# Decoder kernel, expert phase: a deeper row ring, one VectorE job behind each tile, and a scatter split around GpSimd's inverses

## The reference

```python
scores = feats @ centroids.T                       # 8192 rows, 8 experts
expert = jnp.argmax(scores, axis=1)
alpha = sigmoid(sum(feats * centroids[expert]))
h = (xs - mu) * rsqrt(var + 1e-5) * g + b          # per expert, xs = feats
y = xs + relu(h @ W1e.T + b1e) @ W2e.T + b2e       # hidden width 512
out = alpha * y[expert] + (1.0 - alpha) * feats
x = _layernorm(x + out)                            # the kernel's result
```

## Time and profile before

| what | value |
|---|---|
| median of three runs | 3524.48 us |
| the profiled execution | 3520.38 us |
| its span in the profile | 3518.5 us |
| granted TensorE clock over the span | 0.959 |
| start of the expert phase in the span | about 3302 us |

### The profile page before, as it was taken

How to read it: one execution, slowest core, us unless ns; L and a number is a source line. 1 busy time by engine, 2 the same in 40 slices (tenths; PEclk the granted TensorE clock), 3 DMA queues, 4 the chain that set the end, 5 groups by cost and what they waited for, 6 DMA issues and landing times. The chain is left out here.

```text
span 3518.5 us, 101747 instructions
## 1 busy us (share of the span) xinstructions
PE 3132.9 (89%) x40973; PEld 1931.2 (55%) x40973; DVE 2410.5 (69%) x5699; ACT 1967.9 (56%) x3510; POOL 2064.2 (59%) x1842
## 2 busy tenths in 40 slices
PE   6888888877999999898999999999999989999676
PEld 2433444433555556665666666665555545666575
DVE  5999999994555555585665556677888855666465
ACT  5666666652566666432666654335555536666354
POOL 5888888884787877663111114556777742343365
PEclk8999999998999999998999998999999989999798
DMA  4222222225600000000000000000000000000364
GB/s 143 103 90 91 96 100 92 89 88 195 217 2 2 2 2 2 16 1 13 4 5 5 5 3 6 8 8 2 2 2 2 2 17 24 21 17 14 98 175 116
DMA packets 50327, 165.42 MB, mean 47 GB/s; under 512 B 11822, under 2 KB 23217, under 8 KB 40784
## 3 DMA queue, kind: packets, MB, share of 16 engines
q1 hardware_dynamic: 45520, 150.43, 13.1%
q0 software_dynamic: 4352, 8.47, 0.7%
HBM read 149.89 MB, written 43.65 MB: 55 GB/s over the span
## 5 line engine op out<-in xcount | busy, mean ns | idle before, releaser
L530 DVE TENSOR_TENSOR_SCAN XC<-ssm_dA,ssm_db 128x2048 f32<-128x2048 f32 x128 | 565.2, 4416 | 55.6 <-PE ssm_db L374 55.6
L479 ACT ACTIVATE ssm_dA<-ssm_delta,ssm_nega 128x508 f32<-128x508 f32 x512 | 326.0, 707 | 165.9 <-DVE XC L530 162.6
L1229 POOL TENSOR_TENSOR self_pm<-self_pT,weights 128x512 f32<-128x512 f32 x256 | 322.6, 1294 | 54.4 <-ACT self_pT L953 53.0
L594 POOL TENSOR_TENSOR XC<-XC,XB 128x1536 f32<-128x1536 f32 x64 | 253.3, 3958 | 87.9 <-DVE XC L530 87.9
L1235 POOL TENSOR_TENSOR XC<-XC,XB 128x128 f32<-128x128 f32 x128 | 58.5, 458 | 391.6 <-DVE XB L1111 391.6
L594 POOL TENSOR_TENSOR ssm_hC<-XC,XB 128x1536 f32<-128x1536 f32 x64 | 251.8, 3934 | 36.6 <-DVE XC L530 36.6
L374 PE MATMUL ssm_db<-XB,ssm_dxT 32*128 32x128 f32 x4096 | 157.0, 292 | 103.3 <-DVE XC L530 88.9
L374 PEld LDWEIGHTS ssm_db<-XB,ssm_dxT 32*128 32x128 f32 x4096 | 131.7, 193 | 203.8 <-DVE XC L530 183.9
L1097 DVE TENSOR_REDUCE self_nmax<-self_scores 128x4 f32<-128x512 f32 x256 | 158.0, 679 | 82.0 <-PE self_scores L830 81.8
L2663 POOL TENSOR_TENSOR XC<-XC,weights 128x512 f32<-128x512 f32 x128 | 161.8, 1285 | 73.1 <-ACT XC L2497 73.1
L2671 POOL TENSOR_TENSOR XC<-XC,weights 128x512 f32<-128x512 f32 x128 | 161.4, 1283 | 49.7 <-ACT XC L2506 49.5
(11 more groups left out here) (454 smaller groups left out, 8354.3 us busy)
## 6 DMA issues: line engine op xcount, KB each, us to landing
XB<-c_rows SPq DMA_DIRECT2D x64, 1024.0 KB
sorted<-in_padding SPq DMA_DIRECT2D x1, 33280.0 KB, 109.2
experts_we<-in_w_experts SPq DMA_DIRECT2D x72, 323.0 KB, 3.1
experts_rt<-sorted SPq DMA_DIRECT2D x72, 65.0 KB
ssm_xT<-in_xT SPq DMA_DIRECT2D x16, 256.0 KB
XC<-in_w_experts SPq DMA_DIRECT2D x9, 256.0 KB
weights<-in_w_self SPq DMA_DIRECT2D x1, 1412.0 KB, 7.3
cross_ctx_t<-in_ctx SPq DMA_DIRECT2D x16, 77.0 KB
```

The costliest lines, as they stand in the source:

```text
L479: o = act.activation(dA[:, p % 2, :].rearrange("p (b k t) -> p b k t", b=GROUP, k=4)[:, :, k, 1:T], by_batch(delta[:, slot, half, :])[:, : ...
L530: dve.tensor_tensor_scan(states(p).rearrange("p m t -> p (m t)"), dA[:, p % 2, :], db[:, :], 0.0, ALU.mult, ALU.add).then_inc(h_ready, 1)
L594: pool.tensor_tensor(weighted(p).rearrange("p (b k) t -> p b k t", k=4)[:, :, 0:3, :], states(p).rearrange("p (b k) t -> p b k t", k=4)[:, ...
L1229: pool.tensor_tensor(pm[:, n % 2, r, :].rearrange("p (h t) -> p h t", h=4), pT[:, n % 2, r, :].rearrange("p (h t) -> p h t", h=4), bcast(V ...
```

## The change

The ring of fetched rows holds six quads in place of four, and rows are fetched four quads ahead in place of three. The index tile `idx` gets a ring of its own, of eight quads. VectorE's four jobs are spread over the quad: `head_a(q + 2)` behind tile 0, `finish_b(q - 1)` behind tile 1, `head_b(q + 2)` behind tile 2, `finish_a(q)` behind tile 3. On GpSimd the fourth transfer of a quad leaves the burst: it is issued one iteration later, between inverse r and inverse z, and the three others stay behind inverse z.

```diff
--- before.py
+++ after.py
@@ -2693,7 +2693,8 @@
     line = table.rearrange("r w -> (r w)")
     HALVINGS = NB.bit_length() - 1
     assert NB == 1 << HALVINGS
-    RT = 4
+    RT = 6
+    IR = 8
     WS = 8
     HS = 3
     small = w.at["w2"][0]
@@ -2709,7 +2710,7 @@
         tile_at = env["tile_at"]
         alpha = ph.sb("alpha", [P, RT, GROUP])
         rt = ph.sb("rt", [P, RT, GROUP, W])
-        idx = ph.sb("idx", [P, RT, GROUP], U32)
+        idx = ph.sb("idx", [P, IR, GROUP], U32)
         statz = ph.sb("statz", [P, 2, GROUP, 6])
         statr = ph.sb("statr", [P, 2, GROUP, 6])
         mvz = ph.sb("mvz", [P, 2, GROUP, 2])
@@ -2753,7 +2754,7 @@
                 sp.dma_start(rt[:, q % RT, b, :], line[bass.ds(place[j] * (P * W), P * W)].rearrange("(p w) -> p w", w=W)).then_inc(rt_in[q % RT], 16)
 
             place = {}
-            for q in range(3):
+            for q in range(4):
                 for j in range(q * GROUP, (q + 1) * GROUP):
                     locate(j)
                     fetch(j)
@@ -2763,9 +2764,9 @@
             for j in range(TILES):
                 if j + WS < TILES:
                     weights(j + WS)
-                if j + 3 * GROUP < TILES:
-                    locate(j + 3 * GROUP)
-                    fetch(j + 3 * GROUP)
+                if j + 4 * GROUP < TILES:
+                    locate(j + 4 * GROUP)
+                    fetch(j + 4 * GROUP)
             for s in range(2):
                 sp.wait_ge(stored[s], 16 * GROUP * (QUADS // 2))
 
@@ -2857,9 +2858,9 @@
             def head_a(q):
                 dve.wait_ge(rt_in[q % RT], 16 * GROUP * (q // RT + 1))
                 row_stats(dve, lambda b: rt[:, q % RT, b, 0:C], statz[:, q % 2], mvz[:, q % 2], vec_z, q * 2 * GROUP, mark)
-                if q >= RT:
-                    dve.wait_ge(stored[q % 2], 16 * GROUP * ((q - RT) // 2 + 1))
-                dve.tensor_copy(idx[:, q % RT, :], rt[:, q % RT, :, C + 1]).then_inc(idx_ready, 1)
+                if q >= IR:
+                    dve.wait_ge(stored[q % 2], 16 * GROUP * ((q - IR) // 2 + 1))
+                dve.tensor_copy(idx[:, q % IR, :], rt[:, q % RT, :, C + 1]).then_inc(idx_ready, 1)
 
             def head_b(q):
                 dve.wait_ge(pool_z, 2 * q + 2)
@@ -2896,13 +2897,13 @@
                 dve.wait_ge(y_mm, j + 1)
                 dve.scalar_tensor_tensor(r(q % 2)[:, b, :], yp[j % 2][:, 0:C], gate_, here_, ALU.mult, ALU.add)\
                     .then_inc(r_ready, 1)
+                if b == 0 and q + 2 < QUADS:
+                    head_a(q + 2)
                 if b == 1 and q:
                     finish_b(q - 1)
-                if b == 1 and q + 2 < QUADS:
-                    head_a(q + 2)
+                if b == 2 and q + 2 < QUADS:
+                    head_b(q + 2)
                 if b == 3:
-                    if q + 2 < QUADS:
-                        head_b(q + 2)
                     finish_a(q)
             finish_b(QUADS - 1)
 
@@ -2927,11 +2928,11 @@
                     pool.wait_ge(res_ready, q - 1)
                 inv(mvr[:, q % 2], rstdr[:, q % 2], pool_r, q, EPS / 4)
 
-            def scatter(q):
+            def scatter(q, tiles):
                 pool.wait_ge(res_ready, q + 1)
                 pool.wait_ge(idx_ready, q + 1)
-                for b in range(GROUP):
-                    pool.indirect_dma_start(out, bass.IndirectOffsetOnAxis(ap=idx[:, q % RT, b:b + 1], axis=0),
+                for b in tiles:
+                    pool.indirect_dma_start(out, bass.IndirectOffsetOnAxis(ap=idx[:, q % IR, b:b + 1], axis=0),
                                             res(q % 2)[:, b, :], None, bounds_check=NB * P - 1, oob_is_err=False)\
                         .then_inc(stored[q % 2], 16)
 
@@ -2940,12 +2941,15 @@
             for q in range(QUADS):
                 if q:
                     finish(q - 1)
+                if q >= 2:
+                    scatter(q - 2, (3,))
                 if q + 2 < QUADS:
                     head(q + 2)
                 if q:
-                    scatter(q - 1)
+                    scatter(q - 1, (0, 1, 2))
             finish(QUADS - 1)
-            scatter(QUADS - 1)
+            scatter(QUADS - 2, (3,))
+            scatter(QUADS - 1, range(GROUP))
```

## The result

The changed kernel takes **3493.47 us** (median of 4 runs, 3488.87 to 3495.0), beside 3522.41 us for the kernel before (4 runs): a ratio of 0.9919, 95% interval [0.9904, 0.9934]. The forecast was 3488 us. The span of the profiled execution is 3490.8 us.

The account below looks back on a forecast made before the run. Two waits, VectorE's for TensorE and GpSimd's for VectorE, filled 10.52 us iterations; 8.2 (SyncE) over 15 gave -34.8, the last two -2: -37 from 3520.4 made 3483.5, plus 4.1 for the median, 3488 us; range 3479 to 3509.

Parts of the forecast that it names:

- likeliest case: Expert phase: an iteration of 7.97 to 8.6 us, saving 40 to 31 us, so 3484 to 3494 us; chance 65%.
- first rival: Bursts of three still delay TensorE's signals and VectorE waits: 8.8 to 9.96 us an iteration, 3499 to 3516 us; chance 17%.
- Shortening one alone would win little: VectorE's r wait for TensorE (2.65 us) and GpSimd's inverse z wait for VectorE (2.54 to 2.8) close at the same moment.
- instead of 8.2: Iteration of the expert phase: from 10.52 us to SyncE's occupied time, 8.2, over 15 iterations: -34.8 us.
- hidden but for a few tenths: VectorE's r: TensorE's signal, up to 2.3 us late, is mostly covered by VectorE's jobs, now one behind each tile.
- 3.1 us of cover: From r of tile j - 2 VectorE asks for TensorE's result two jobs and one tile later; worst case wants 3.4.
- The three transfers need `finish_b`: GpSimd's burst: its normalisation is made while inverse z is computed, so GpSimd can run without idle time, 7.97 us.
- its stretches double: Rival: each of two bursts an iteration stretches SyncE's instructions as one did, 9.8 us an iteration, 3514 us; chance 5%.
- the single transfer brings late signals of its own: Rival, slower: VectorE is held twice an iteration, 12.3 us, +26 us or 3551 us; chance 6%.
- GpSimd's floor: GpSimd's iteration without idle time: 1.57 + 1.12 + 1.61 + 3.67 = 7.97 us for inverses and transfers.
- third rival: VectorE's normalisations hold GpSimd for their whole length through the shared port: 9.1 us an iteration, 3503 us; chance 3%.
- the forecast's 2: Last two iterations: the single transfer fills 1.12 us of GpSimd's wait for VectorE, once each: -2 us.

Follow-up runs that it names:

- e_three_banks: The changed kernel with three PSUM output banks instead of two, so TensorE may run one tile further ahead: ratio 0.9876 to before, 8.12 us an iteration.
- a_split_only: The changed kernel (deeper rings and fetch, split burst) with VectorE's jobs in their old order: ratio 0.9924 to before, 9.40 us an iteration.
- b_jobs_only: The changed kernel (deeper rings and fetch, new VectorE order) with GpSimd's burst of four back: ratio 0.9975 to before, 10.02 us an iteration.
- g_in_order: The changed kernel with GpSimd's indirect transfers replaced by plain ones in tile order, writing rows to wrong places: one run, 3469.06 us, 7.61 us an iteration.
- m_in_order_again: The changed kernel with plain transfers in tile order, repeated on a fourth chip: one run, 3478.01 us, 7.65 us an iteration.

## Why the prediction was right, and where its terms were off

**Right in sign and in both savings, wrong about what is left.** The forecast was 37 us less and 29 came, which lies just inside its likeliest case (3484 to 3494). Both halves of it took their part: inverse z no longer waits for VectorE, and half of what VectorE waited for TensorE lies behind its jobs. But neither SyncE nor GpSimd bounds the iteration, as it had it; the ring through the late signal does, which is its first rival. Two of its own signs of being wrong stand in the trace, r still waiting over 1 us for TensorE in every iteration and GpSimd idle before its three transfers, and 8.64 us lies just outside its 7.97 to 8.6. The total is right partly by luck: 3493.5 us is as near to the 3499 of the first rival as to its own 3488.

The sentence "Shortening one alone would win little" was wrong: the split alone gave 19.8 us, the order alone 5.9. The burst is a term of the one ring that holds both waits, and the split shortens it.

**The iteration: 8.64 us instead of 8.2.** This term is off by 0.44 x 15 = 6.6 us, of the 8 us missing. Two steps of it were too small.
- *"I take it that the lateness is hidden but for a few tenths."* 1.25 us stay, nearly one half of 2.65. The forecast counted 3.1 us of cover from the moment the bank is free (r of tile j - 2), as if TensorE began the group at once. By the rows of one iteration VectorE asked even later, at 3389.71, 3.7 us behind that r (3386.02), but TensorE began only at 3388.07, 2.05 us behind it, since its groups stand in a queue. The cover that counts is from the group's end, 3389.13, to VectorE's asking, 0.58 us; the lateness was 1.9. So the first rival, half of the lateness exposed (8.8 us), was nearer to what happened inside the iteration than the forecast's own step. Its 8.8 is 0.16 too much since VectorE's work and gaps are 8.64 - 1.25 = 7.4 us and not 7.66.
- *"The three transfers need `finish_b`, which comes one tile later, while inverse z is computed."* It ends while inverse z does (3394.40 and 3394.44), but a transfer starts 0.80 us behind the normalisation that it waited for, 0.20 behind GpSimd's own instruction. 0.57 us an iteration, which no term held. It is no second loss: both stand in one ring, in which the late r pushes the normalisation.

**SyncE: right in size, wrong as the bound.** It waits 0.6 of 8.64 us, so it is occupied for about 8.0, forecast 8.2; with 8.12 an iteration in e_three_banks it still waited. It never decided. The rival that its stretches double fell with that, and so did the one that the single transfer brings late signals of its own: r waits for TensorE once an iteration, as before.

**GpSimd's floor** of 7.97 us was 0.13 too low. The power of z, which now stands beside a normalisation, took 1.14 us on average over 14, that of r 1.04:

```profile
L2917 POOL TENSOR_TENSOR experts_rstdz<-experts_rstdz,experts_power 128x4 f32<-128x4 f32 x14 | 16.0, 1143 | 1.2
L2917 POOL TENSOR_TENSOR experts_rstdr<-experts_rstdr,experts_power 128x4 f32<-128x4 f32 x14 | 14.6, 1043 | 1.2
```

That is the third rival's price: 0.1 us, not 1.1. The power of z (3393.27 to 3394.44) and a whole normalisation of 1.11 us (3393.29 to 3394.40) ran side by side. The Trainium skill ("SBUF — State Buffer", SBUF: two separate sides) says that VectorE in a two-port mode and GpSimd lock one port pair for a whole instruction and that the other fully blocks. No run here shows such a block, though no row tells whether the normalisation ran in that mode.

**The last two iterations** gave 0.7 us instead of 2: 9.03 + 6.87 = 15.9 after 16.57. The split alone took them to 13.74 (a_split_only), the new order alone to 18.27 (b_jobs_only), both on a chip with late signals; where none was late they took 13.87 (e_three_banks) and 13.75 (g_in_order). So the forecast's 2 were in the split, and VectorE's new order, which the forecast gave no term here, took most of them back; why it does so only where signals are late is not shown.

**The start and the clock.** The later weights cost nothing in total, as forecast (25.5 us to the first inverse r), though ScalarE did wait for them once, 2.10 us at 3329.71. The stretches at 1.2 GHz that the forecast allowed for did not come: the granted clock is 1.00 from 3320 to 3460.

**The larger rings** cost nothing, but they are not the free extra that the forecast made of them: in d_three_ahead, with the quads of rows back at four and the fetch at three ahead, the phase is 0.9 us longer than before the change. The forecast asked when the statistics would be wanted, and not whether their rows would be there.

**What is open.** Why the second chip held no signals; whether it is the chip or the loading of the program (on no chip did both kinds show among the kernels with indirect transfers, which speaks for the chip); and what the kernel before and the changed kernel take there, since neither was profiled on it (of before its median there is 3517.91 us, elsewhere 3520.11 to 3526.57). So the share of the third bank in e_three_banks' 8.12 us is not known either: where signals are held it is zero.

## What to carry to other kernels

Count the cover of a late signal from the end of the work that it reports to the moment when the waiting engine would ask, and not from when a buffer comes free. An order that moves a consumer earlier needs its inputs fetched earlier by as much; try the order without the deeper fetch before calling the fetch free. And repeat the winner beside its rival on the same chip: a kernel that by its ratio to before was 0.4% ahead on one chip was level on the next, and only the pair told that.

## What the runs showed of the hardware

- TensorE's signals are held while GpSimd issues a burst of indirect transfers, mostly by 2.3 us before and 1.9 us after the change (2.3 at most) and by some 3.3 us in b_jobs_only, and the r that waits starts mostly 0.8 to 1.0 us behind the burst's end (1.3 at most). This was so in nine profiles on at least three chips, and in neither of the two profiles with such bursts on one other chip. SyncE's instructions stretch with it. The plainest sign is the MOVE ahead of a fetch, 0.03 us at the median: it reaches 0.71 us in the changed kernel and 0.04 in e_three_banks (below, source line L2754 from 3335 to 3435: least, median and most in ns), and in all nine profiles some register instruction of SyncE took 0.70 us or more, in the other five none over 0.16. A long DMA instruction is no such sign: e_three_banks has one of 1.69 us.

```profile
L2754 SPq MOVE experts_rt<-sorted x47: 6/29/711, 3336.3 to 3434.4; - x47
```

```profile
L2754 SPq MOVE experts_rt<-sorted x49: 29/29/37, 3336.3 to 3429.6; - x49
```

- GpSimd's plain transfers of the same tiles take 0.62 us, and three in a row 1.70, where indirect ones took 1.10 and 3.66; no signal was held beside them in g_in_order, whose lines these are, nor in m_in_order_again:

```profile
3384.41 1.70 POOL L2936 DMA_DIRECT2D out<-XB  x3 [0.50 <-DVE XB L141]
...
3389.47 0.62 POOL L2936 DMA_DIRECT2D out<-XB  x1
```
